# A two-layer transformer on one core: the second layer's q and k projected once, the rotary partner fetched by transfers

## The chip, the core and the metric

One core of a Trainium2 chip runs the whole program. The metric is the device time of one execution in microseconds; where several runs are compared, the median. Engines: PE (TensorE, matmuls and transposes), DVE (VectorE), ACT (ScalarE), POOL (GpSimd), SP (SyncE, which issues every DMA of this program). Each engine works through its own instructions strictly in order, and an instruction waits on semaphores that others raise.

## The reference

Two layers over x of 2 batches x 512 tokens x 256. Each layer is a layer norm, attention, a residual sum, a layer norm, a mixture of 16 experts and one shared expert, and a residual sum. Layer 0's attention has 16 heads of 128, layer 1's 16 heads of 16. What the change touches is the start of layer 1's attention:

```python
def rotate_half(x):
    half = x.shape[-1] // 2
    x1, x2 = (x[..., :half], x[..., half:])
    return jnp.concatenate([-x2, x1], axis=-1)

def apply_rope(x, base=BASE):
    ...
    return x * jnp.cos(emb) + rotate_half(x) * jnp.sin(emb)
```

q = x Wq + bq and k = x Wk + bk, both [2, 512, 256], both through apply_rope within each head of 16, then softmax(q k^T / 4) v and the output projection. Row i of a head and row i + 8 are each other's partners.

## The kernel before

All matmul inputs of the projections and experts are split into a high and a low part ("hi", "lo": ACT writes hi as a copy in the matmul's format, DVE or POOL writes the difference), and each product is three matmuls: hi by hi, lo by hi, hi by lo, over two chunks of 128 channels. So one projection of 128 output rows by 512 tokens is 6 matmuls of 128x128 weights by 512 columns.

The program is six stretches, one after the other: layer 0 attention, its 34 expert items ("rows", i = 0 to 33, `row_pe`, `row_act`, `row_dve`, `row_pool`: 17 experts for batch 0, then 17 for batch 1), layer 1 attention as 32 "steps" (`a1_pe`, `a1_act`, `a1_dve`, `a1_pool`, `a1_sp`), and its experts. The order on every engine is written out by hand; tables say at which row or step a side job stands.

A row i on PE is gate(i) and up(i) (6 matmuls of 512 columns each, L955 and L964) and down(i-2) (12 matmuls of 256 columns, L978). On ACT it is hid_high(i-1) (L1054), silu(i) (L1035), ew_high(i+2) (L1068), then side jobs. On DVE: hid_low(i-1), gated(i) (gu, L1153), side jobs. On POOL: weighted(i) (guw, L1118), ew_low(i+2) (L1102), side jobs. From row 20 on all rows use the same two PSUM banks for gate and up, so gate(i+1) waits until silu(i) has read its bank, and up(i+1) until gated(i) has.

Layer 1's q and k come in 8 groups g = (t, mt, h), with t = q or k, mt = a half of the 256 channels, h = the batch. Groups 0 to 3 (batch 0) are side jobs of rows 21 to 27, groups 4 to 7 (batch 1) of steps 4 to 11. The rotation is done by projecting twice: w1 holds q's weights, q's weights with each head's halves exchanged ("sw" = 1), the same for k, and v. For each group `group_pe` (L1517) runs 2 x 6 matmuls (L1527); `group_dve` (L1816) makes rc = (projection + bias) * cos and rs = (exchanged projection + bias) * sin out of PSUM; `rotated` on POOL (L1778) adds them to rr; `high` on ACT (L1688) and `low` (L1768; DVE for groups 0 to 3, POOL for 4 to 7) split rr; `stack` on SP (L1455) writes both to DRAM, from where `load` (L1459) brings pairs of heads back, stacked for the steps.

A step s of layer 1 attention: for each of 4 heads a slot j with one score matmul for the step (L1646, ks by qs, with 3 banks, so that matmul n waits for the exponential n - 2) and one maximum matmul for 7 steps later (L1550, read by DVE L1838); then 4 slots x 1 value matmul of the step before (L1616), which open the next step. ACT does the 4 exponentials (L1733) and then the step's side jobs. At s % 4 = 0 ACT also reads out the values, at s % 4 = 1 PE also turns maxima and values. Batch 1's layer norm is: `ln_stats(2, 1)` on DVE in step 0, rstd and xn on POOL (L265, L242), transposes by PE at the end of step STEP_T1 = 3, its groups from step 4.

Where the tables stand:

```python
ROW_GROUP = {21: ((0, 0), (0, 1)), 22: ((1, 0), (1, 1)), 23: ((2, 0), (2, 1)), 24: ((3, 0),), 25: ((3, 1),)}
ROW_V = {25: 0, 26: 1}
ROW_HIGH = {22: 0, 23: 1, 24: 2, 26: 3}
STEP_HIGH = {5: 4, 6: 5, 9: 6, 11: 7}
```

## Time and profile before

| | us |
|---|---|
| median of 3 runs | 871.23 |
| lowest and highest | 865.35, 877.39 |
| the profiled execution | 863.91 |
| its span, first to last instruction | 862.2 |
| PE busy in the span | 824.2 (96%) |
| DVE, ACT, POOL busy | 649.3, 525.4, 465.4 |

The span lies 1.7 us below the profiled execution's own time. A PE matmul's duration runs from its issue to its modelled end and overlaps the next one, so its price in a dense stretch is the distance between starts. "Idle before" in brackets is how long the engine stood before an instruction, and what released it.

### The profile page before, as it was taken

Reading aid. Unit: us, or ns where it says so; the run is one execution under the profiler, and the core shown is the slowest. Engines: PE = TensorE matmul, PEld = TensorE weight load, DVE = VectorE, ACT = ScalarE, POOL = GpSimd, SP = SyncE. Lnnn points to the kernel's source line nnn. Section 1 sums busy time; section 2 is a strip of 40 time slices with the busy share of each in tenths; the row PEclk is TensorE's granted clock in tenths of the full one; section 3 lists DMA queues with packets and bytes.
Section 4 is the critical chain, followed back from the end, with each engine's and each line's share of the span. In section 5 each row is a group of like instructions: output and inputs, shape, how many; then the busy total and the mean of one; then the engine's idle time right before and its main releaser. Section 6 shows DMA issues by size and latency. Waiting matters only on the chain.

```text
span 862.2 us, 14797 instructions
## 1 busy us (share of the span) xinstructions
PE 824.2 (96%) x4544; PEld 624.0 (72%) x4544; DVE 649.3 (75%) x1350; ACT 525.4 (61%) x1106; POOL 465.4 (54%) x399
## 2 busy tenths in 40 slices
PE   8899999999999999989998999999999889999997
PEld 6678788777878888866887888654444347888886
DVE  5898888899998888998386866868788544676553
ACT  4778788777878888773534442346566464454442
POOL 4555555665665556642666766533201326656774
PEclk9999999999999999999999999999999899999999
DMA  5232233332423223212764458312431132334441
GB/s 157 93 98 92 94 97 97 111 97 67 151 87 98 97 92 105 80 50 75 218 214 156 141 164 292 106 58 91 145 111 50 57 99 93 123 125 142 151 162 65
DMA packets 57442, 99.20 MB, mean 115 GB/s; under 512 B 8288, under 2 KB 19040, under 8 KB 57376
## 3 DMA queue, kind: packets, MB, share of 16 engines
q1 hardware_dynamic: 57376, 98.39, 35.6%
q8 instruction: 33, 0.54, 0.3%
q14 instruction: 33, 0.27, 0.1%
HBM read 71.88 MB, written 9.57 MB: 94 GB/s over the span
## 4 chain that ended last, share of the span: by engine, by line
PE 63%; issue 10%; POOL 10%; DVE 10%; ACT 4%; DMA 3%; SPq 1%; DVEq 0%; POOLq 0%; ACTq 0%
PE ps L978 10%; PE ps L964 10%; PE ps L955 9%; PE ps L321 6%; PE ps L386 5%; PE ps L332 4%; POOL q_sin L530 3%; PE ps L345 3%; PE ps L374 3%; PE ps L1646 3%; PE ps L1527 2%; PE ps L359 2%; POOL wqk_lo L517 2%; PE ps L1616 2%; DVE nm L1838 2%
## 5 line engine op out<-in xcount | busy, mean ns | idle before, releaser
L1102 POOL TENSOR_TENSOR ew_lo<-ew_raw,ew_hi 128x768 fp32r<-128x768 f32 x68 | 128.1, 1885 | 60.0 <-ACT ew_hi L1068 52.0
L1054 ACT ACTIVATE hid_hi<-guw 128x512 fp32r<-128x512 f32 x68 | 43.0, 632 | 156.1 <-POOL guw L1118 106.2
L1157 DVE TENSOR_TENSOR hid_lo<-guw,hid_hi 128x512 fp32r<-128x512 f32 x68 | 80.7, 1187 | 72.1 <-ACT hid_hi L1054 72.0
L1118 POOL TENSOR_TENSOR guw<-gu,cwb 128x512 f32<-128x512 f32 x61 | 80.4, 1319 | 91.1 <-issue 73.8
L530 POOL TENSOR_TENSOR q_sin<-q_sw,sin 128x512 f32<-128x512 f32 x64 | 83.4, 1311 | 52.5 <-DMA q_sw<-q_in 51.1
L1838 DVE TENSOR_REDUCE nm<-ps 128x1 f32<-128x512 f32 x128 | 81.3, 683 | 19.6 <-PE ps L1550 18.3
L1733 ACT ACTIVATE e<-ps 128x512 f32<-128x512 f32 x128 | 68.8, 601 | 35.4 <-PE ps L1646 35.2
L978 PE MATMUL ps<-ew_hi,hid_hi 128*128 128x256 f32 x272 | 78.3, 288 | 2.4 <-DVE hid_lo L1157 1.8
L509 DVE SCALAR_TENSOR_TENSOR w<-ex,rden,sgn 128x512 f32<-128x512 f32 (+3 forms) x128 | 78.0, 670 | 0.0
L437 ACT ACTIVATE ex<-sabs,nmax 128x512 f32<-128x512 f32 (+3 forms) x128 | 61.5, 551 | 27.1 <-DVE nmax L483 27.1
L978 PE MATMUL ps<-ew_lo,hid_hi 128*128 128x256 f32 x272 | 76.8, 282 | 0.0
L978 PE MATMUL ps<-ew_hi,hid_lo 128*128 128x256 f32 x272 | 76.8, 282 | 0.0
L332 PE MATMUL ps<-q_rot 128*128 128x512 f32 (+3 forms) x256 | 74.5, 433 | 1.1 <-DVE v L462 1.1
L386 PE MATMUL ps<-wT,v 128*128 128x512 f32 (+3 forms) x256 | 74.3, 433 | 1.0 <-ACT wT L422 1.0
L478 DVE TENSOR_TENSOR q_rot<-ps,q_sin 128x512 f32<-128x512 f32 x64 | 43.6, 688 | 39.5 <-POOL q_sin L530 24.6
L386 PEld LDWEIGHTS ps<-wT,v 128*128 128x128 f32 x256 | 46.3, 190 | 26.8 <-issue 16.6
L396 ACT ACTIVATE q_in<-ps,bqkv 128x512 f32<-128x512 f32 x64 | 43.8, 687 | 32.5 <-PE ps L321 32.4
L332 PEld LDWEIGHTS ps<-q_rot 128*128 128x128 f32 x256 | 43.4, 190 | 27.7 <-issue 16.6
L414 ACT ACTIVATE sgn<-ps 128x512 bf16<-128x512 f32 (+3 forms) x128 | 59.8, 468 | 0.0
L955 PE MATMUL ps<-xT_hi,ew_hi 128*128 128x512 f32 x136 | 55.7, 410 | 3.6 <-issue 3.6
L412 ACT ACTIVATE sabs<-ps 128x512 f32<-128x512 f32 (+3 forms) x128 | 58.7, 459 | 0.0
L1646 PE MATMUL ps<-qs,ks 50*128 50x512 f32 x128 | 51.5, 467 | 7.2 <-ACT e L1733 7.2
(189 smaller groups left out, 2397.3 us busy)
## 6 DMA issues: line engine op xcount, KB each, us to landing
ew_raw<-in_ew SPq DMA_DIRECT2D x68, 384.0 KB, 3.5
q_sw<-q_in SPq DMA_DIRECT2D x128, 128.0 KB, 2.0
cwb<-cw_dram SPq DMA_DIRECT2D x61, 256.0 KB, 3.7
wqk_raw<-in_wqk SPq DMA_DIRECT2D x32, 256.0 KB, 2.7
wv_raw<-in_wv SPq DMA_DIRECT2D x32, 128.0 KB, 2.6
wo_raw<-in_wo SPq DMA_DIRECT2D x32, 128.0 KB, 2.2
qs<-stk_q SPq DMA_DIRECT2D x16, 256.0 KB, 3.3
ks<-stk_k SPq DMA_DIRECT2D x16, 256.0 KB, 3.8
```

The lines of the kernel that those rows point to most:

```text
L332: pe.matmul(ps[:, bank, col:col + P * (qi + 1)], q_rot[:, par(1), 0, qi * P:(qi + 1) * P], q_rot[:, par(1), 1, 0:P * (qi + 1)], start=True ...
L386: last = pe.matmul(ps[:, 7, j * P:S], v0[:, slot_of(0), j, odd() * DH0:(odd() + 1) * DH0], wT[:, j, j * P:S], start=j == 0, stop=j == QT - ...
L509: dve.scalar_tensor_tensor(out=w[:, qi, ROW[qi]], in0=ex[:, qi, ROW[qi]], scalar=rden[:, qi:qi + 1], in1=sgn[:, par(1), qi, ROW[qi]], op0= ...
L530: pool.tensor_tensor(q_sin[:, t, :], q_sw[:, t, :], sin0[:, :], ALU.mult).then_inc(sem("q_sin"), 1)
L955: last = pe.matmul(ps[:, gu_pair(f, i)[0], :], ff[f].ew[pw][:, i % EW_SLOTS, c * P:(c + 1) * P], half_of((xT_hi, xT_lo)[px][:, c, :], h), ...
L964: last = pe.matmul(ps[:, gu_pair(f, i)[1], :], ff[f].ew[pw][:, i % EW_SLOTS, (DC + c) * P:(DC + c + 1) * P], half_of((xT_hi, xT_lo)[px][:, ...
L978: last = pe.matmul(ps[:, Y_BANK[f, h][t // 2], t % 2 * D:(t % 2 + 1) * D], ff[f].hid[px][:, i % 2, t * P:(t + 1) * P], ff[f].ew[pw][:, i % ...
L1102: pool.tensor_tensor(ff[f].ew[1][:, i % EW_SLOTS, :], ew_raw[:, i % RAW_SLOTS, :], fp(ff[f].ew[0][:, i % EW_SLOTS, :]), ALU.subtract).then ...
L1118: pool.tensor_tensor(ff[f].guw[:, i % 2, :], ff[f].gu[:, i % 2, :], ff[f].cwb[:, r % CWB_SLOTS, :], ALU.mult).then_inc(sem("guw"), 1)
L1157: dve.tensor_tensor(ff[f].hid[1][:, i % 2, :], ff[f].guw[:, i % 2, :], fp(ff[f].hid[0][:, i % 2, :]), ALU.subtract).then_inc(sem("hid_lo"), 1)
L1646: pe.matmul(ps[:, S_BANK[n % S_BANKS], :], ks[rows, slot_at, kt * P:(kt + 1) * P], qs[rows, slot_at, :], start=True, stop=True).then_inc(s ...
L1838: dve.tensor_reduce(nm1[:, quad % 2, col:col + 1], ps[:, BANK_OF["max", n], :], AX.X, ALU.max, negate=True).then_inc(sem("max"), 1)
```

## The change

- w1 holds 3 parts instead of 5 (q, k, v), loaded in 4 transfers instead of 6, split in rows 11, 13 and 15 instead of 11 to 19. `w1_parts` writes q's and k's columns interleaved (h i s), so that a row and its partner stand on neighbouring partitions; the tables cos, sin and b1 are loaded in that order, in 6 transfers instead of 3.
- Each group is projected once, by 6 matmuls. `evict` on ACT adds the bias and writes the group from PSUM to qe. `swap_halves` on SP copies qe to qw with even and odd partitions exchanged, in two transfers. `turned` on POOL makes rs = qw * sin. `group_dve` makes rc out of PSUM, and now waits for `evict`. `rotated` adds, on DVE in the rows and on POOL in the steps.
- Groups run in pairs: matmuls in rows 21 and 23 and in steps 3 and 6; `turned`, `rotated` and `high` of a pair one row later, in one row; in the steps `high` stands at the end of steps 5 and 8.
- v is projected in rows 22 and 24 instead of 25 and 26.
- `ln_stats(2, 1)` moves from step 0 to the end of the rows, STEP_T1 from 3 to 2.

```diff
-        ROW_GROUP = {21: ((0, 0), (0, 1)), 22: ((1, 0), (1, 1)), 23: ((2, 0), (2, 1)), 24: ((3, 0),), 25: ((3, 1),)}
-        ROW_V = {25: 0, 26: 1}
-        ROW_HIGH = {22: 0, 23: 1, 24: 2, 26: 3}
+        ROW_GROUP = {21: (0, 1), 23: (2, 3)}
+        ROW_TURN = {22: (0, 1), 24: (2, 3)}
+        ROW_V = {22: 0, 24: 1}
+        ROW_LOW = {23: (0, 1), 25: (2, 3)}
...
-        STEP_T1 = 3
+        STEP_T1 = 2
+        STEP_GROUP = {(3, 1): 4, (3, 3): 5, (6, 1): 6, (6, 3): 7}
+        STEP_HIGH = {5: (4, 5), 8: (6, 7)}
...
+        def swap_halves(sp, g):
+            sp.wait_ge(sem("qk1_ev"), g + 1)
+            wait(sp, "rs", g - 1)
+            for o in range(2):
+                sp.dma_start(qw[o:P:2, g % 2, :], qe[1 - o:P:2, g % 2, :]).then_inc(sem(f"qk1_sw{g % 2}"), 16)
...
             maxima(sp, 1)
             loads_after(sp, 0)
+            swap_halves(sp, 4)
+            swap_halves(sp, 5)
             maxima(sp, 2)
             stack(sp, 4)
             stack(sp, 5)
+            swap_halves(sp, 6)
+            swap_halves(sp, 7)
             sp.wait_ge(sem("stk_st"), 16 * 3 * 6)
             loads_after(sp, 1)
...
+        def evict(act, g):
+            t, mt, h = GROUPS1[g]
+            act.wait_ge(sem("qk1_ps"), g + 1)
...
+            act.activation(qe[:, g % 2, :], ps[:, BANK_OF["qk", g], :], ACT.Identity,
+                           bias=b1[:, 2 * t, mt:mt + 1]).then_inc(sem("qk1_ev"), 1)
...
-            if i in ROW_HIGH:
-                high(act, ROW_HIGH[i])
+            for g in ROW_TURN.get(i, ()):
+                high(act, g)
+            for g in ROW_GROUP.get(i, ()):
+                evict(act, g)
...
-        def rotated(pool, g):
-            pool.wait_ge(sem("rs"), 2 * (g + 1))
-            wait(pool, "qk1_hi", g - 1)
+        def turned(pool, g):
+            pool.wait_ge(sem(f"qk1_sw{g % 2}"), 32 * (g // 2 + 1))
+            wait(pool, "rr", g - 1)
+            pool.tensor_tensor(rs[:, g % 2, :], qw[:, g % 2, :], sin1[:, :], ALU.mult).then_inc(sem("rs"), 1)
+
+        def rotated(eng, g):
+            eng.wait_ge(sem("rs"), g + 1)
+            eng.wait_ge(sem("qk1_cos"), g + 1)
+            wait(eng, "qk1_hi", g - 1)
...
-            for g in range(4, 8):
-                rotated(pool, g)
-                low(pool, g)
-                if g == 5:
+            for g in range(4, 8, 2):
+                for step in (turned, rotated, low):
+                    step(pool, g)
+                    step(pool, g + 1)
+                if g == 4:
                     x_bias(pool, 1)
...
+                for g in ROW_LOW.get(i, ()):
+                    low(dve, g)
+                for g in ROW_GROUP.get(i, ()):
+                    group_dve(dve, g)
                 if i in ROW_V:
                     v_dve(dve, ROW_V[i])
-                if i in ROW_HIGH:
-                    low(dve, ROW_HIGH[i])
+                for g in ROW_TURN.get(i, ()):
+                    rotated(dve, g)
```

ACT in the rows, before, from row 22's hid_hi on (hid_hi, gu and ew_hi are one row's three jobs, qk_hi<-rr is `high`):

```order
L1054 ACTIVATE hid_hi<-guw_124 128x512 [waits y,guw]
L1035 ACTIVATE gu_123<-ps 128x512 [waits guw,gate]
L1068 ACTIVATE ew_hi<-ew_raw 128x768 [waits y,ew_ld0]
L1688 ACTIVATE qk_hi<-rr 128x512 [waits rr]
L1054 ACTIVATE hid_hi<-guw_124 128x512 [waits y,guw]
L1035 ACTIVATE gu_123<-ps 128x512 [waits guw,gate]
L1068 ACTIVATE ew_hi<-ew_raw 128x768 [waits y,ew_ld1]
L1688 ACTIVATE qk_hi<-rr 128x512 [waits rr]
```

and of the changed kernel, from row 22's hid_hi on (qe is what `evict` writes):

```order
L1054 ACTIVATE hid_hi<-guw_126 128x512 [waits y,guw]
L1035 ACTIVATE gu_125<-ps 128x512 [waits guw,gate]
L1068 ACTIVATE ew_hi<-ew_raw 128x768 [waits y,ew_ld0]
L1713 ACTIVATE qk_hi<-rr 128x512 [waits rr] x2
L1054 ACTIVATE hid_hi<-guw_126 128x512 [waits y,guw]
L1035 ACTIVATE gu_125<-ps 128x512 [waits guw,gate]
L1068 ACTIVATE ew_hi<-ew_raw 128x768 [waits y,ew_ld1]
L1705 ACTIVATE qe<-ps,b_99 128x512 [waits qk1_sw0,qk1_ps]
L1705 ACTIVATE qe<-ps,b_99 128x512 [waits qk1_sw1,qk1_ps]
```

Before, one `high` closed each of rows 22 and 23. Now row 22 closes with two and row 23 with two `evict`s; row 24 closes with the other two `high`s, row 25 with nothing.

POOL in the rows, before, rows 21 and 22 (guw is `weighted`, ew_lo is `ew_low`, rr is `rotated`):

```order
L1118 TENSOR_TENSOR guw_124<-gu_123,cwb_122 128x512 [waits hid_lo,gu,cwb_ld1]
L1102 TENSOR_TENSOR ew_lo<-ew_raw,ew_hi 128x768 [waits ew_hi_act]
L1778 TENSOR_TENSOR rr<-rc,rs 128x512 [waits rs]
L1118 TENSOR_TENSOR guw_124<-gu_123,cwb_122 128x512 [waits hid_lo,gu,cwb_ld2]
L1102 TENSOR_TENSOR ew_lo<-ew_raw,ew_hi 128x768 [waits ew_hi_act]
L1778 TENSOR_TENSOR rr<-rc,rs 128x512 [waits rs]
```

and of the changed kernel, rows 21 to 23 (rs is `turned`):

```order
L1118 TENSOR_TENSOR guw_126<-gu_125,cwb_124 128x512 [waits hid_lo,gu,cwb_ld1]
L1102 TENSOR_TENSOR ew_lo<-ew_raw,ew_hi 128x768 [waits ew_hi_act]
L1118 TENSOR_TENSOR guw_126<-gu_125,cwb_124 128x512 [waits hid_lo,gu,cwb_ld2]
L1102 TENSOR_TENSOR ew_lo<-ew_raw,ew_hi 128x768 [waits ew_hi_act]
L1814 TENSOR_TENSOR rs<-qw,sin_98 128x512 [waits qk1_sw0]
L1814 TENSOR_TENSOR rs<-qw,sin_98 128x512 [waits qk1_sw1]
L1118 TENSOR_TENSOR guw_126<-gu_125,cwb_124 128x512 [waits hid_lo,gu,cwb_ld0]
```

One operation in each of rows 21 to 23 and 25 has become two in row 22 and two in row 24, and the sum is DVE's.

ACT in the steps, before, from the second half of step 4 to the first half of step 8 (e is an exponential, zst the read-out, nmT the turned maxima):

```order
L1733 ACTIVATE e_157<-ps 128x512 [waits pv1,st_ps] x6
L1693 ACTIVATE nmT<-ps 32x128 [waits nm_st0,nmT_ps]
L1688 ACTIVATE qk_hi<-rr 128x512 [waits stk_st,rr]
L1733 ACTIVATE e_157<-ps 128x512 [waits pv1,st_ps] x4
L1688 ACTIVATE qk_hi<-rr 128x512 [waits rr]
L1733 ACTIVATE e_157<-ps 128x512 [waits pv1,st_ps] x6
```

and of the changed kernel, steps 3 to 7:

```order
L1770 ACTIVATE e_159<-ps 128x512 [waits pv1,st_ps] x4
L1705 ACTIVATE qe<-ps,b_99 128x512 [waits qk1_sw0,qk1_ps]
L1705 ACTIVATE qe<-ps,b_99 128x512 [waits qk1_sw1,qk1_ps]
L1770 ACTIVATE e_159<-ps 128x512 [waits pv1,st_ps] x2
L1727 ACTIVATE zst<-ps 128x512 [waits pv1]
L1770 ACTIVATE e_159<-ps 128x512 [waits pv1,st_ps] x6
L1718 ACTIVATE nmT<-ps 32x128 [waits nm_st0,nmT_ps]
L1713 ACTIVATE qk_hi<-rr 128x512 [waits stk_st,rr]
L1713 ACTIVATE qk_hi<-rr 128x512 [waits rr]
L1770 ACTIVATE e_159<-ps 128x512 [waits pv1,st_ps] x4
L1705 ACTIVATE qe<-ps,b_99 128x512 [waits qk1_sw0,qk1_ps]
L1705 ACTIVATE qe<-ps,b_99 128x512 [waits qk1_sw1,qk1_ps]
```

Two `evict`s now stand between the exponentials of steps 3 and 4 and of steps 6 and 7, and two `high`s behind those of step 5 (and of step 8), where single `high`s stood behind steps 5, 6, 9 and 11.

## Rows read from the trace of the kernel before

**Rows 1.** The page: busy time of each engine, its share of the span, instructions.

```profile
PE 824.2 (96%) x4544; PEld 624.0 (72%) x4544; DVE 649.3 (75%) x1350; ACT 525.4 (61%) x1106; POOL 465.4 (54%) x399
```

**Rows 2.** Windows: expert rows 21 to 26, attention steps 1 to 11.

```profile
core 0: us, PE busy (x) PEld busy (x) DVE busy (x) ACT busy (x) POOL busy (x), PEclk, DMA share, GB/s
...
487.44:526.95 39.51, 39.51 (x219) 34.15 (x218) 24.25 (x29) 14.69 (x24) 26.77 (x18) 1.00 0.62 198
...
576.75:623.25 46.50, 43.72 (x248) 20.35 (x247) 37.03 (x64) 26.75 (x53) 18.09 (x14) 1.00 0.33 106
```

**Rows 3.** Timeline of PE, row 22 (start, duration, engine, line).

```profile
494.56 0.39 PE L955 MATMUL ps<-xT_hi,ew_hi 128*128 128x512 f32 x1
...
497.35 0.39 PE L1527 MATMUL ps<-xT_hi,w_hi 128*128 128x512 f32 x1
...
500.13 0.28 PE L978 MATMUL ps<-ew_hi,hid_hi 128*128 128x256 f32 x1
...
501.57 0.39 PE L955 MATMUL ps<-xT_hi,ew_hi 128*128 128x512 f32 x1
```

**Rows 4.** Timeline of ACT and POOL, rows 22 and 23.

```profile
496.15 0.60 ACT L1035 ACTIVATE gu<-ps 128x512 f32<-128x512 f32 x1 [0.70 <-PE ps L955]
...
498.44 1.29 POOL L1118 TENSOR_TENSOR guw<-gu,cwb 128x512 f32<-128x512 f32 x1 [1.82 <-issue]
...
499.69 1.86 POOL L1102 TENSOR_TENSOR ew_lo<-ew_raw,ew_hi 128x768 fp32r<-128x768 f32 x1
```

**Rows 5.** Timeline of POOL and DVE, row 21: two operations that meet.

```profile
489.12 1.86 POOL L1102 TENSOR_TENSOR ew_lo<-ew_raw,ew_hi 128x768 fp32r<-128x768 f32 x1
...
489.87 1.66 DVE L1157 TENSOR_TENSOR hid_lo<-guw,hid_hi 128x512 fp32r<-128x512 f32 x1 [0.66 <-ACT hid_hi L1054]
```

**Rows 6.** Layer 0's exchange; DMA issues (KB each, us to landing).

```profile
224.51 0.69 ACT L396 ACTIVATE q_in<-ps,bqkv 128x512 f32<-128x512 f32 x1 [0.70 <-PE ps L321]
...
227.60 2.55 POOL L530 TENSOR_TENSOR q_sin<-q_sw,sin 128x512 f32<-128x512 f32 x2 [0.49 <-DMA q_sw<-q_in]
...
q_sw<-q_in SPq DMA_DIRECT2D x128, 128.0 KB, 2.0
...
w_raw<-in_w SPq DMA_DIRECT2D x6, 256.0 KB, 5.9
```

**Rows 7.** Timeline of PE, attention steps (L1616 opens each step).

```profile
584.76 1.09 PE L277 MATMUL ps<-ident,xn 128*128 128x128 f32 x8
...
588.01 0.50 PE L1527 MATMUL ps<-xT_hi,w_hi 128*128 128x512 f32 x1
...
589.61 0.50 PE L1646 MATMUL ps<-qs,ks 50*128 50x512 f32 x1
...
598.04 1.07 PE L1616 MATMUL ps<-e,vx 128*32 128x512 f32 x8
...
600.65 1.07 PE L1616 MATMUL ps<-e,vx 128*32 128x512 f32 x8
...
638.26 1.06 PE L1616 MATMUL ps<-e,vx 128*32 128x512 f32 x8
...
641.53 1.06 PE L1616 MATMUL ps<-e,vx 128*32 128x512 f32 x8
...
644.86 1.07 PE L1616 MATMUL ps<-e,vx 128*32 128x512 f32 x8
```

**Rows 8.** Timeline of DVE and POOL, step 0: norm of batch 1.

```profile
574.81 1.39 DVE L231 BATCH_NORM_STATS2 stats<-x 128x6 f32<-128x256 f32 x4
...
576.76 1.02 POOL L265 TENSOR_TENSOR rstd<-vareps,minus_half 128x4 f32<-128x4 f32 x1 [11.35 <-DVE vareps L236]
```

**Rows 9.** Timeline of DVE in step 24, and two windows there.

```profile
671.44 4.26 DVE L1843 TENSOR_TENSOR nm_s<-nm 128x16 fp32r<-128x16 f32 x1
...
671.00:675.00 4.00, 2.37 (x14) 0.67 (x12) 3.90 (x2) 3.03 (x6) 4.00 (x3) 0.99 0.00 0
...
675.00:681.80 6.80, 5.66 (x17) 2.34 (x21) 2.76 (x6) 1.19 (x3) 0.67 (x1) 0.50 0.28 84
```

124 lines of the change are left out of this document (67 added, 57 removed).

## The prediction

> **What bounds the kernel now.** I read the page's busy line first, then the windows of the two stretches that the change touches, then PE's timeline in them, then the engines behind PE. PE is busy for 96% of the span [rows 1]. In rows 21 to 26 it has no idle time at all: 39.51 us busy of 39.51 [rows 2]. So there a matmul removed is time won, as long as nothing else becomes late. In the attention steps 1 to 11 PE is busy for 43.72 of 46.50 us, with DVE at 37.03 and ACT at 26.75 [rows 2]: PE still leads, with less room. A row of two projections lasts 501.57 - 494.56 = 7.01 us, of which gate and up take 2.79, the twelve projection matmuls 2.78 and the downs 1.44 [rows 3]. One 512-column matmul is thus worth 2.78 / 12 = 0.232 us.
>
> **What is removed.** 8 groups x 6 matmuls = 48, worth 11.1 us at 0.232. They fall in two halves. In the rows, 24 x 0.232 = 5.6 us. The two v jobs (12 matmuls of 256 columns, as the downs, 1.44) only change places. In the steps a group of six takes 589.61 - 588.01 = 1.60 us [rows 7], so four are worth 6.4.
>
> **Rows 21 to 26: what is late next.** Before, one `high` closed a row on ACT and found its input ready. Now a pair goes through weighted, ew_low, `turned` twice (POOL), `rotated` twice (DVE) and `high` twice (ACT) within one row, and ACT cannot take up the next row's silu before it. For row 22: POOL ends weighted and ew_low at 499.69 + 1.86 = 501.55 [rows 4]. Two `turned` at layer 0's rate for the same operation (2.55 for two, [rows 6]) end at 504.1. `rotated` meets a lock: hid_lo, a subtraction of two SBUF operands on DVE, met a POOL operation that ended at 490.98 and itself ended at 491.53, 0.55 later, after 1.66 us [rows 5]. So the first `rotated` ends at 504.65, 0.55 behind the second `turned`, and the second at 505.2. Two `high`s and hid_high (0.6 each) end at 506.3 with some overlap, silu (0.60, [rows 4]) at 506.85, 12.3 us after the row's start. Gate of row 24 needs that silu. Rows 22 and 23 on PE last 7.01 - 2.78 + 1.44 = 5.67 and 7.01, so row 24 starts at 507.2: covered, by 0.4 us. The same chain starts again in row 24, where 5.67 and an empty row of 4.23 lie in front of row 26's gate: 9.9 us against 12.3, a stall of 2.4. It grows because DVE reaches row 24 late: in row 23 it makes two `low`s, each held by a POOL operation in the same way [rows 5], and two rc's behind `evict`, which moves gated(24) some 2 us. I take 4.5 us (ends: 2.4 without that lag, 5 with a slower exchange), and 0.6 more for ew_low(27), which waits for row 25's weighted. Rows: 5.6 - 4.5 - 0.6 = 0.5 us saved instead of 5.6. The exchange itself is hidden there: `evict` of group 1 ends at about 494.0, in layer 0 the data was there 227.60 - 225.20 = 2.4 us after the eviction [rows 6], and POOL asks at 501.5. At 5.9, the slowest kind of transfer in the list [rows 6], it is hidden too.
>
> The lock between DVE and POOL is also what the Trainium skill describes (SBUF — State Buffer, section "SBUF: two separate sides"): a DVE operation with two SBUF inputs and a reading POOL operation exclude each other for a whole instruction. By it `rotated` on DVE beside `turned` on POOL is not parallel work; rows 5 agree with their 1.66 us. Without the lock the chain would be 0.5 us shorter and DVE not late in row 24: a stall of 1.9 us instead of 4.5, and 863.7 instead of the sum below.
>
> **Steps 1 to 11.** Without stalls I add the new steps up from rows 7: six plain ones at 600.65 - 598.04 = 2.61 (15.7), two with a read-out at 641.53 - 638.26 = 3.27 (6.5), two with turned maxima at 644.86 - 641.53 = 3.33 (6.7), one with four more transposes, estimated at 2.9, the layer norm's transposes 1.1, four groups 6.4. Sum 39.3 against 46.50 [rows 2], 7.2 saved; the removed groups are 6.4 of it, the rest is a wait for a load that the earlier stacking should end.
>
> Against that stand the new waits on ACT. (a) `evict` of groups 5 and 7 (0.69 us, the shape of layer 0's q_in, [rows 6]) stands ahead of the next step's first exponential, which PE's score matmul needs: 0.35 us each, 0.7. (b) `high` of groups 4 and 5 at the end of step 5. Counted from the start of step 4: `evict` done at 0.8, exchange landed at 3.8 (2.4 in rows 6, plus the queue on SP), second `turned` 5.1, two `rotated` 7.6, second `high` 8.2, first exponential of step 6 at 8.8. PE wants it at 8.0: 0.8 us. (c) `high` of groups 6 and 7 at the end of step 8, two steps after the pair's, which are only 2.6 + 0.35 + 3.3 = 6.2 us long: by the same count the exponential comes at 8.7, and PE wants it at 7.2: 1.5 us. DVE waits for `evict` too, with maxima behind it, but four PSUM banks lie between. Steps: 7.2 - 0.7 - 0.8 - 1.5 = 4.2 us saved.
>
> **Small things.** ln_stats(2, 1) leaves step 0, where it kept POOL waiting 11.35 us [rows 8]. Its 2 us (1.39 for the sums, [rows 8], and the small operations) go to the end of the rows, ahead of two maxima that PE does not need for four slots: nothing there, about 0.2 won at the maxima of step 0. Two splits of w1 leave ACT and DVE in rows 17 and 19, where PE hardly waits: 0 to 0.3. The interleaved split of q and k has no row; it lies under experts with the same element count: 0, at most 1 us if strides slow it. Three more issues on SP in row 14 stand ahead of an expert's load that is used three rows later: 0.
>
> **Sum.** 0.5 + 4.2 + 0.2 = 4.9 us. The profiled execution took 863.91, so 859.0 in its terms. It lies 7.3 below the median of the three runs, 871.23; in their terms 866.3.
>
> **Rivals.**
> 1. The stalls are not there: ACT's queue has slack that I miss. Then rows and steps give 5.6 + 7.2 less a little, 12: 859.3. For it: PE without idle time in rows 21 to 26 [rows 2] with ACT at 14.69 of 39.51. Against: ACT's slack is no help to what stands behind a wait in its own queue.
> 2. PE's clock falls in row 26. In step 24 a DVE operation was held 4.26 us; PE was busy 2.37 of 4.00 us there, and in the next 6.80 us the granted clock was 0.50, the lower level of 1.2 GHz [rows 9]. A stall of 4.5 us in row 26 has the same form. Some 4.4 of such 6.8 us would fall on matmuls at half speed and cost 2.2, of which 0.6 hides the wait for ew_low(27): 1.6 less saved, and with a second such gap in step 9 3.3: 869.6 at the far end. The Trainium skill has the same rule (TensorE: Matmul & The Clock Gate, section "Why this matters for your kernels"): idle gaps between bursts return the array to the lower clock. Rows 9 agree, with 0.50.
> 3. The exchange is slow in the steps, and the kernel becomes slower. If it lands 7 us after `evict` (5.9 from issue, as w_raw's loads, [rows 6], plus issue) and not 3, ACT's `high` behind steps 5 and 8 holds all exponentials 4 us longer, twice: 8 us, and two idle gaps of 5 us bring the clock down, 3 us more: 11 - 4.9 = 6.1 slower, 877.3. It turns the sign when landing takes more than about 5.4 us. Against it: q_sw lands in 2.0 [rows 6], and the steps have less DMA work (share 0.33) than the rows (0.62) [rows 2].
>
> **Chances.** The forecast (saved 2.5 to 7 us) 0.5, rival 1 0.2, rival 2 0.15, rival 3 0.12, anything else 0.03. The range, from rival 1 with its interval to rival 3 with most of its, and the scatter of runs, 857.5 to 877. About 2% can be told from no change for this kernel. 2% is 17.4 us: more than all matmuls removed and every wait won (about 13), so faster by over 2% gets only the runs' scatter, 0.03; slower by over 2% needs rival 3 with more than twice its price, 0.04; within 2% 0.93.
>
> **What would show it.** In the new profile: ACT idle in front of `high` in rows 22 and 24, about 7 us each time, released by DVE's rr; PE idle before row 26's gate for 2 to 5 us; idle in front of the score matmuls of steps 6 and 9; 48 projection matmuls of q and k instead of 96; half clock near row 26 or not. PE dense through row 26 with row 27's gate 5.6 us earlier would refute my main step; exchanges landing over 5 us would point to rival 3.

## The result, and the profile after

The changed kernel takes 878.64 us (median of 10 runs, 868.51 to 882.45) against 870.41 (10 runs, 864.55 to 877.39): ratio 1.0107, 95% interval 1.0063 to 1.0151. It is slower by about 1%, 8.2 us by the medians. The ratio is taken from the fast executions; three of the changed kernel's ten were slow ones, over 1.5% above its fastest, and without them its median is 876.35. The profiled execution took 876.35 us with a span of 874.2, against 863.91 and 862.2. These two lie 12.4 us apart, 4 more than the medians, since the profiled execution of the kernel before was quicker than any of the ten.

The page's busy line (compare [rows 1]) shows the 48 matmuls gone from PE (4496 for 4544) and its share two points lower:

```profile
PE 824.9 (94%) x4496; PEld 622.6 (71%) x4496; DVE 647.7 (74%) x1344; ACT 529.6 (61%) x1112; POOL 470.3 (54%) x403
```

PE is busy as long as before with fewer matmuls. Windows of the changed kernel tell why: first the two that answer to [rows 2] (rows 21 to 26, steps 1 to 11, from the same instructions), then three stretches at half clock.

```profile
core 0: us, PE busy (x) PEld busy (x) DVE busy (x) ACT busy (x) POOL busy (x), PEclk, DMA share, GB/s
488.64:531.51 42.87, 36.06 (x195) 31.15 (x194) 25.46 (x29) 16.94 (x28) 25.38 (x17) 0.92 0.63 202
581.24:635.50 54.26, 45.75 (x225) 18.88 (x224) 37.61 (x60) 29.94 (x59) 19.14 (x15) 0.78 0.35 117
...
522.70:529.50 6.80, 4.21 (x10) 3.37 (x11) 5.45 (x7) 4.71 (x8) 3.38 (x2) 0.50 0.98 358
597.80:604.60 6.80, 6.08 (x29) 2.05 (x21) 6.24 (x10) 4.03 (x9) 5.42 (x5) 0.50 0.01 2
618.30:635.30 17.00, 12.55 (x49) 5.33 (x49) 7.75 (x13) 8.82 (x18) 5.71 (x5) 0.50 0.33 105
```

The 12.0 us between the spans lie so: 1.2 before row 21 (1.5 up to row 0, in code that the change leaves alone and where the clock fell twice for 3.4 us, then 0.3 won), 42.87 - 39.51 = 3.4 in rows 21 to 26, nothing from row 27 to step 1, 54.26 - 46.50 = 7.8 in steps 1 to 11, nothing behind them.

**The rows.** Timeline of the changed kernel in rows 23 to 26:

```profile
511.48 1.41 SPq L1457 DMA_DIRECT2D stk_k<-qk_lo  x1
513.00 5.10 SPq L1463 DMA_DIRECT2D qw<-qe  x4
...
519.85 2.48 POOL L1814 TENSOR_TENSOR rs<-qw,sin 128x512 f32<-128x512 f32 x2 [2.56 <-DMA qw<-qe]
521.14 2.34 DVE L1824 TENSOR_TENSOR rr<-rc,rs 128x512 f32<-128x512 f32 x2 [6.49 <-POOL rs L1814]
522.91 1.23 ACT L1713 ACTIVATE qk_hi<-rr 128x512 fp32r<-128x512 f32 x2 [10.37 <-DVE rr L1824]
524.57 0.58 ACT L1035 ACTIVATE gu<-ps 128x512 f32<-128x512 f32 x1
525.29 0.76 PE L955 MATMUL ps<-xT_hi,ew_hi 128*128 128x512 f32 x1 [6.80 <-ACT gu L1035]
```

Read it upwards: the gate of row 26 (L955) waits 6.80 us for silu, silu stands behind `high` (L1713), which waits 10.37 us for `rotated`, that for `turned`, and that for the exchange, which SP issues behind the stacks of groups 0 and 1 and which has landed by 519.85. Row 26 then runs at half clock and takes 6.22 us instead of 4.23. So: -5.6 for the matmuls, +6.8 for the stall, +2.0 for the clock; that is 3.2 of the 3.4.

**The steps.** Timeline of the changed kernel in steps 8 and 9:

```profile
608.82 1.80 SPq L1457 DMA_DIRECT2D stk_k<-qk_lo  x1
609.59 0.69 ACT L1705 ACTIVATE qe<-ps,b 128x512 f32<-128x512 f32 x1 [1.56 <-PE ps L1543]
610.72 4.37 SPq L1463 DMA_DIRECT2D qw<-qe  x4
616.63 2.49 POOL L1814 TENSOR_TENSOR rs<-qw,sin 128x512 f32<-128x512 f32 x2 [9.40 <-DMA qw<-qe]
620.36 0.63 ACT L1713 ACTIVATE qk_hi<-rr 128x512 fp32r<-128x512 f32 x1 [4.87 <-POOL rr L1824]
622.12 1.07 ACT L1770 ACTIVATE e<-ps 128x512 f32<-128x512 f32 x2
622.75 0.79 PE L1662 MATMUL ps<-qs,ks 50*128 50x512 f32 x1 [5.71 <-ACT e L1770]
```

SP issues both exchanges from 610.72 on, behind the stacks. Group 6's lands at 616.6, 8.5 us behind its `evict`; `evict` of group 7 ends at 610.28 and its exchange lands at 617.4, 7.1 us later. ACT holds step 9's exponentials behind `high` of 6 and 7; PE waits 5.71 us. Step 9 takes 10.32 us (3.33 for a step of its kind), and 10 and 11, at half clock, 5.20 and 4.00 instead of 2.9 and 2.6. Step 5 shows another wait, on DVE:

```profile
597.25 1.28 POOL L1814 TENSOR_TENSOR rs<-qw,sin 128x512 f32<-128x512 f32 x1 [0.37 <-DMA qw<-qe]
598.48 2.50 POOL L1824 TENSOR_TENSOR rr<-rc,rs 128x512 f32<-128x512 f32 x2
598.55 1.24 DVE L1887 TENSOR_TENSOR nm_s<-nm 128x16 fp32r<-128x16 f32 x1
599.82 1.19 DVE L1889 TENSOR_TENSOR nm_s<-nm,nm_s 128x16 fp32r<-128x16 f32 x1
601.07 0.40 PE L1572 MATMUL ps<-ident,nm_s 128*32 128x128 f32 x1 [0.71 <-DVE nm_s L1889]
```

Two products of 16 columns, 0.17 us each where POOL is idle, take 1.24 and 1.19 beside POOL's operations, and PE's next instruction needs them. Step 5 takes 5.90 instead of 3.33. PE stands 0.71 us of that; the rest is at half clock, which began at 597.8, ahead of both products. Where step 5 ran at full clock with the same order (rows_high_late, high67_at_10_loads, loads_first, warm_26), PE stood 1.8 us there and the step took 5.17 to 5.20.

### The profile page after: what moved, and what is told of

The parts are those of the page before. It is cut to its first block and busy times, and to the rows that moved or that the text cites. A ratio compares the mean times of both kernels' runs of the same rounds, so it can differ in the third digit from the quotient of the medians.

```text
span 874.2 us, 14742 instructions
## 1 busy us (share of the span) xinstructions
PE 824.9 (94%) x4496; PEld 622.6 (71%) x4496; DVE 647.7 (74%) x1344; ACT 529.6 (61%) x1112; POOL 470.3 (54%) x403
## 5 line engine op out<-in xcount | busy, mean ns | idle before, releaser
L1157 DVE TENSOR_TENSOR hid_lo<-guw,hid_hi 128x512 fp32r<-128x512 f32 x68 | 78.6, 1156 | 71.8 <-ACT hid_hi L1054 71.6
L1662 PE MATMUL ps<-qs,ks 50*128 50x512 f32 x128 | 55.3, 497 | 13.4 <-ACT e L1770 13.3
L955 PE MATMUL ps<-xT_hi,ew_hi 128*128 128x512 f32 x136 | 56.3, 414 | 10.5 <-ACT gu L1035 6.8
L1662 PEld LDWEIGHTS ps<-qs,ks 50*128 50x128 f32 x128 | 22.7, 200 | 59.9 <-ACT e L1770 47.8
```

Source lines behind the costliest of these rows:

```text
L955: last = pe.matmul(ps[:, gu_pair(f, i)[0], :], ff[f].ew[pw][:, i % EW_SLOTS, c * P:(c + 1) * P], half_of((xT_hi, xT_lo)[px][:, c, :], h), ...
L1157: dve.tensor_tensor(ff[f].hid[1][:, i % 2, :], ff[f].guw[:, i % 2, :], fp(ff[f].hid[0][:, i % 2, :]), ALU.subtract).then_inc(sem("hid_lo"), 1)
L1662: pe.matmul(ps[:, S_BANK[n % S_BANKS], :], ks[rows, slot_at, kt * P:(kt + 1) * P], qs[rows, slot_at, :], start=True, stop=True).then_inc(s ...
```

## The experiments

Each is compared with the kernel before, run on the same chip; the changed kernel's ratio is 1.0107. The changed kernel itself was run in one set only, in which the kernel before had a median of 870.41, against 865.05 to 866.60 in the sets below; of the kernels made from it, all_three, all_four and all_five alone have intervals that lie wholly under its own. Since the clock also falls in places that no edit touches (last section), two stretches of each trace stand beside the ratio: row 21's gate to row 33's, and the start of step 2 to that of step 14.

| kernel | ratio (95%) | rows 21-33 | steps 2-14 |
|---|---|---|---|
| before | 1 | 72.80 | 53.49 |
| changed | 1.0107 (1.0063-1.0151) | 76.12 | 61.30 |
| rows_high_late | 1.0140 (1.0082-1.0198) | 73.44 | 62.71 |
| steps_high_late | 1.0292 (1.0241-1.0343) | 76.28 | 72.73 |
| both_high_late | 1.0245 (1.0184-1.0307) | 73.67 | 72.49 |
| no_exchange | 1.0046 (1.0003-1.0089) | 73.15 | 56.05 |
| rows_turn_25 | 1.0061 (1.0027-1.0095) | 73.47 | 61.71 |
| high67_at_10 | 1.0126 (1.0044-1.0207) | 76.02 | 61.52 |
| high67_at_10_loads | 1.0033 (0.9991-1.0074) | 76.13 | 58.01 |
| swap_pool_queue | 1.0099 (1.0058-1.0140) | 76.07 | 60.90 |
| rows_sum_25 | 1.0068 (1.0032-1.0104) | 71.61 | 59.82 |
| loads_first | 1.0060 (1.0027-1.0092) | 76.54 | 53.61 |
| sum_after_nm | 1.0165 (1.0117-1.0214) | 76.55 | 61.94 |
| all_three | 1.0008 (0.9975-1.0041) | 71.59 | 54.45 |
| before_less | 0.9950 (0.9922-0.9979) | 68.12 | 53.88 |
| warm_26 | 1.0159 (1.0097-1.0220) | 74.95 | 65.86 |
| all_four | 0.9989 (0.9959-1.0020) | 71.24 | 57.24 |
| all_five | 0.9995 (0.9961-1.0030) | 71.04 | 53.73 |
| before_less_early | 0.9917 (0.9883-0.9951) | 68.12 | 48.85 |
| before_early | 0.9967 (0.9936-0.9998) | 72.81 | 52.18 |

How far one trace's stretch can be trusted is seen where an edit leaves its code alone. Rows 21 to 33 took 76.02 to 76.55 us in the six kernels whose edit lies in the steps only. Steps 2 to 14 took 59.82 to 62.71 in three whose edit lies in the rows only (warm_26, with its clock down in steps 0 to 2, 65.86): in kernels made from the changed one, a difference under 3 us there says little.

**First: are the highs only too early?** rows_high_late:

```diff
-            for g in ROW_TURN.get(i, ()):
+            for g in ROW_TURN.get(i - 1, ()):
                 high(act, g)
```

> ScalarE makes the two high parts of groups 0, 1 in row 23 and of groups 2, 3 in row 25, a row later than in the changed kernel; nothing else moves. Theory A (the highs stand too early on ScalarE): in the changed kernel's trace the gate matmul of row 27 stands 4.6 us later than before the change and that of row 25 0.1 us earlier, so 4.7 us are lost to the wait for row 24's highs, half of it stall (TensorE idle 6.80 us in front of row 26's gate), half of it clock at 0.5 for 6.8 us. Then this kernel is 4 to 5 us faster than the changed one, TensorE has no wait over 1 us in front of row 26's gate and the granted clock stays at full speed there. Theory B (fewer matmuls keep TensorE thin, so the clock falls with or without a stall): the clock falls near row 26 all the same and the gain is 2 to 3 us. Theory C (the highs only wait in another row): the stall of 4 to 7 us stands before row 25's or 27's gate, gain under 1 us.

Measured: row 24's gate to row 28's 25.88 us (28.55 in the changed kernel), so 2.7 won, and half clock from 520.5 all the same. The wait had gone to the next engine, as its timeline shows:

```profile
516.93 2.51 POOL L1814 TENSOR_TENSOR rs<-qw,sin 128x512 f32<-128x512 f32 x2 [2.57 <-DMA qw<-qe]
518.25 2.34 DVE L1824 TENSOR_TENSOR rr<-rc,rs 128x512 f32<-128x512 f32 x2 [6.33 <-POOL rs L1814]
521.11 0.68 DVE L1153 TENSOR_TENSOR gu<-gu,ps 128x512 f32<-128x512 f32 x1
521.84 0.80 PE L964 MATMUL ps<-xT_hi,ew_hi 128*128 128x512 f32 x1 [3.60 <-DVE gu L1153]
```

DVE's product of gate and up stands behind `rotated`. A is half right, C names the rest. The ratio does not show the 2.7; the two intervals leave room for it.

This run's steps are those of the changed kernel, and they show a wait that the changed kernel's own trace hides:

```profile
636.10 0.51 PE L1566 MATMUL ps<-ks,qs 48*128 48x512 f32 x2 [1.96 <-DMA ks<-stk_k]
```

The loads behind the stacks of groups 6 and 7 are late for step 13, which takes 9.73 us instead of 4.96. In the changed kernel PE comes later to it, since steps 10 and 11 ran at half clock (5.20 and 4.00 us, here 3.51 and 2.73). The three other kernels with unedited steps show 8.10, 6.19 and 10.34. So 4.96 is no measure for the experiments below, and part of the half clock behind step 9 covers this wait.

steps_high_late has this edit, and both_high_late has it beside that of rows_high_late:

```diff
-        STEP_HIGH = {5: (4, 5), 8: (6, 7)}
+        STEP_HIGH = {6: (4, 5), 10: (6, 7)}
```

> ScalarE makes the highs of groups 4, 5 behind the exponentials of step 6 (5 in the changed kernel) and those of groups 6, 7 behind step 10's (8). Theory A: from step 9's value matmuls to step 12's the changed kernel takes 19.5 us and the kernel before 13.6; the 5.9 us are the 5.71 us that TensorE waits for step 9's exponentials behind the highs of groups 6, 7 and the half clock after it, less the two projections gone there. Then this kernel is 5 to 7 us faster than the changed one and steps 9 to 12 run at full clock. Theory B (thin TensorE): half clock of 15 us or more stays between steps 5 and 12, gain 2 to 3 us, the stall's share alone. Theory C (the wait moves to a later step): TensorE waits 3 us or more for exponentials in step 11, gain under 2 us.

> The two edits together. Theory A: the two gains add, 9 to 12 us under the changed kernel, which is 1 to 3 us under the kernel before. Theory B: 4 to 6 us under the changed kernel, still 2 to 4 us above the kernel before. Theory C: under 3 us.

All three theories fall: steps 2 to 14 took 11.4 us longer than in the changed kernel. `high` of groups 4 and 5 came at 608.5, so their stacks were issued until 615.8, the exchange of groups 6 and 7 from 615.9, the loads at 620.6, and step 9's maxima waited 4.8 us for these loads. What stands on SP is one chain: stacks of one pair, exchange of the next, loads. A `high` that is late for ACT's good is late for all of it.

**Second: the exchange itself.** no_exchange leaves the exchange out:

```diff
-            pool.wait_ge(sem(f"qk1_sw{g % 2}"), 32 * (g // 2 + 1))
+            pool.wait_ge(sem("qk1_ev"), g + 1)
...
-            pool.tensor_tensor(rs[:, g % 2, :], qw[:, g % 2, :], sin1[:, :], ALU.mult).then_inc(sem("rs"), 1)
+            pool.tensor_tensor(rs[:, g % 2, :], qe[:, g % 2, :], sin1[:, :], ALU.mult).then_inc(sem("rs"), 1)
...
-                swap_halves(sp, g)
```

> Leaves out the exchange of partner rows: the sine product reads the evicted rows themselves, and the 32 transfers and their waits are gone; all else as in the changed kernel. Theory D (the exchange is what is late): in row 24 GpSimd's sine product then starts 2.6 us earlier, so the stall before row 26's gate falls from 6.8 to about 4.3 us; in step 8 it starts 5.7 us earlier (at about 611 instead of 616.6), so the highs are ready when ScalarE comes to them and step 9's stall of 5.7 us and its half clock are gone: 7 to 9 us faster in all. Theory A' (the engines' chain of sine product, sum and high is too long by itself): both stalls stay over 3 us, gain 2 to 4 us. Theory B: gain 2 us or less, half clock remains.

The row 26 stall is 4.2 us (forecast of D 4.3; my prediction, with the exchange hidden, 4.5), and step 9 takes 4.33 us instead of 10.32. The exchange is worth 3.0 us in the rows and 5.3 in the steps, 8.2 together, where theory D expected 7 to 9; the ratios give 5.3 us, with overlapping intervals. So it is the traces that show D. Step 5's two products took 0.18 and 0.17 us here. Step 13 took 9.71 us, as long as it can take with unedited steps.

swap_pool_queue issues the exchanges of groups 4 to 7 from POOL:

```diff
-            swap_halves(sp, 4)
-            swap_halves(sp, 5)
-            swap_halves(sp, 6)
-            swap_halves(sp, 7)
...
-                for step in (turned, rotated, low):
+                for step in (swap_halves, turned, rotated, low):
```

> The exchanges of groups 4 to 7 are issued by GpSimd, which waits for them anyway, instead of SyncE, where those of groups 6, 7 stand behind the stacks of groups 4, 5; the rest is the changed kernel. Theory S: the exchange of group 6 starts at its eviction (608.0 on the changed kernel's scale instead of 610.7) and that of group 7 at 610.3, so the sums are ready 2 to 4 us earlier and step 9's stall of 5.7 us falls to 2 to 4: 2 to 5 us faster than the changed kernel. Rival Q (the time is in the transfer itself and in GpSimd's issue, not in the queue it stands in): stall over 5 us, within 1.5 us of the changed kernel or slower.

Timeline of POOL in it:

```profile
606.56 1.12 POOL L1463 DMA_DIRECT2D qw<-qe  x2
608.72 1.09 POOL L1463 DMA_DIRECT2D qw<-qe  x2 [1.04 <-ACT qe L1701]
613.42 1.27 POOL L1810 TENSOR_TENSOR rs<-qw,sin 128x512 f32<-128x512 f32 x1 [3.61 <-DMA qw<-qe]
617.16 1.26 POOL L1810 TENSOR_TENSOR rs<-qw,sin 128x512 f32<-128x512 f32 x1 [2.46 <-DMA qw<-qe]
```

Issued 4 us earlier (these steps run 1.3 us ahead of the changed kernel's), the two exchanges land at 613.3 and 617.1, where the changed kernel has 616.6 and 617.4: group 6's gains, group 7's does not, and PE's stall in step 9 is 6.88 us, over the 5 of rival Q. The DMA issues of POOL (KB each, us to landing) in two windows, 592 to 598 with no stack on its way, and 606 to 618 beside the stacks of groups 4 and 5:

```profile
qw<-qe POOLq DMA_DIRECT2D x4, 128.0 KB, 2.3
```

```profile
qw<-qe POOLq DMA_DIRECT2D x4, 128.0 KB, 5.5
```

The same transfer from the same queue takes 3.2 us longer beside the stacks (six transfers of 256 KB for a pair). So most of its lateness comes with the stacks, and leaving SP's queue does not cure it. What in the stacks slows it is not told apart: the DMA engines' busy share was 0.63 in the changed kernel at that time, not 1.

**Third: loads behind stacks.** high67_at_10 has the first hunk, high67_at_10_loads both:

```diff
-        STEP_HIGH = {5: (4, 5), 8: (6, 7)}
+        STEP_HIGH = {5: (4, 5), 10: (6, 7)}
...
             stack(sp, 6)
-            stack(sp, 7)
             loads_after(sp, 2)
+            stack(sp, 7)
```

> Only the highs of groups 6, 7 move, from behind step 8's exponentials to behind step 10's. Theory S (one queue carries exchange, stacks and loads in one order): step 9's 5.7 us wait for exponentials goes, but the loads issued at step 12 follow the six transfers of 256 KB of groups 6, 7 directly and land late, as in the runs where step 13 took 9.7 us instead of 5.0; so 1 to 4 us faster than the changed kernel, with step 13 at 9 to 12 us. Rival R (only the order on ScalarE matters): step 13 stays at 5 us and the gain is 6 to 9 us.

> The run before with one more edit: the transfers to DRAM of group 7 are issued behind the loads of step 12, as in the kernel before. Theory S: step 13 takes 5 us again and the whole is 6 to 9 us faster than the changed kernel, that is 0 to 2 us slower or faster than the kernel before. Rival R: no difference to the run before it.

Step 9 fell to 5.43 us, step 12 rose to 7.13 and step 13 to 10.29, and nothing was won: R falls. For S step 13 says less than it seems, since with no edit in the steps it also took up to 10.34. With group 7's stacks behind the loads step 13 is 8.28. Still too long: the loads went at 630.9, behind group 6's stacks. loads_first puts both behind (highs of 6, 7 behind step 10 again):

```diff
+            loads_after(sp, 2)
             stack(sp, 6)
             stack(sp, 7)
-            loads_after(sp, 2)
```

> Highs of groups 6, 7 behind step 10 and SyncE issues the loads of step 12 ahead of the stacks of both groups 6 and 7 (with only group 7's behind them step 13 took 8.3 us: the loads were issued at 630.9, behind group 6's stacks). Theory S: the loads are issued 2 us earlier with no stack's bytes in front, step 13 takes 5 to 6 us, and from step 3's value matmuls to step 14's it takes 50 to 51.5 us (changed kernel 57.7, with group 7 alone behind the loads 53.2, kernel before 50.9): 7 to 9 us faster than the changed kernel. Rival (another wait stands there, or step 17 waits for groups 6, 7's stacks instead): over 53 us, or a step of 5 us or more among steps 16 to 19 that took 3.3 before.

Steps 3 to 14 took 49.97 us and step 13 4.96, at full clock and with no wait for loads: S is shown for this stretch. The ratio gives 4 us, not 7 to 9; the profile has 43 us of half clock, 3.4 of them in steps 3 to 14.

**Fourth: the small products.** sum_after_nm:

```diff
                 for step in (turned, rotated, low):
+                    if step is rotated:
+                        pool.wait_ge(sem("nm_lo"), 1 + g // 2)
                     step(pool, g)
```

> The changed kernel with one wait more: GpSimd starts the sums of groups 4, 5 (6, 7) only after VectorE's two small products of the negated maxima of step 4 (8) are done. In the changed kernel these took 1.24 and 1.19 us in step 5 beside GpSimd's sums, against 0.17 each where GpSimd was idle. Theory L (a GpSimd operation on two SBUF tensors holds VectorE's): the second of the two takes 0.2 to 0.4 us again, the first at most what is left of the sine product before it; TensorE's maxima transpose comes 1 us or more earlier in step 5, which takes 4.5 to 5 us instead of 5.9; 1 to 3 us faster than the changed kernel. Rival N (the small products are late for another reason): both stay near 1.2 us, no gain; or the later sums push the highs out and it is slower.

Step 5's products took 0.18 and 0.17 us and step 5 3.33 instead of 5.90: L, with 1.9 us for the wait (5.2 at full clock) and 0.7 for the clock. Then step 6 waits for the first time, 0.81 us for its exponentials behind the highs, and takes 6.66 instead of 6.08:

```profile
603.55 0.49 PE L1662 MATMUL ps<-qs,ks 50*128 50x512 f32 x1 [0.81 <-ACT e L1770]
```

In step 9 POOL's wait stood too late (products 1.10 and 1.19, beside `turned`). The kernel was not faster; its step 13 took 10.22 us, as in others whose step 13 was not touched.

**Fifth: the rows' order.** rows_turn_25 (highs a row late too, stacks of groups 2, 3 in row 27) and rows_sum_25:

```diff
-        ROW_TURN = {22: (0, 1), 24: (2, 3)}
-        ROW_LOW = {23: (0, 1), 25: (2, 3)}
+        ROW_TURN = {22: (0, 1), 25: (2, 3)}
+        ROW_LOW = {23: (0, 1), 26: (2, 3)}
```

> Row 24's sine products and sums of groups 2, 3 move to row 25, their highs to row 26 ahead of that row's evictions (groups 0, 1: row 23), their lows to row 26 and their transfers to DRAM to row 27. In the run that moved the highs alone a row down, the wait moved from ScalarE to VectorE: VectorE held row 25's product of gate and up 3.6 us behind a sum that waited 6.3 us for GpSimd's sine products and these 2.6 us for the exchange. Theory V (the exchange's landing and the sine products reach into row 25's work, so whichever engine holds the next step stalls): with another row between, no engine waits over 1.5 us in front of the gates of rows 25 to 27, the clock stays at full speed, and from row 24's gate to row 27's it takes 18.4 to 19 us as before the change (23.1 in the changed kernel, 20.3 with the highs alone moved): 4 to 5 us faster than the changed kernel. Rival W (the sums on VectorE and sine products on GpSimd hold each other wherever they stand): a wait of 2 to 4 us and a half clock in row 25 or 26, gain 1 to 3 us.

```diff
         ROW_TURN = {22: (0, 1), 24: (2, 3)}
+        ROW_SUM = {22: (0, 1), 25: (2, 3)}
-        ROW_LOW = {23: (0, 1), 25: (2, 3)}
+        ROW_LOW = {23: (0, 1), 26: (2, 3)}
...
+            for g in ROW_GROUP.get(i, ()):
+                swap_halves(sp, g)
             for g in ROW_STACK.get(i, ()):
                 stack(sp, g)
-            for g in ROW_GROUP.get(i, ()):
-                swap_halves(sp, g)
```

> In row 23 the exchange of groups 2, 3 is issued ahead of the stacks of groups 0, 1; the sums of groups 2, 3 on VectorE move from row 24 to row 25 (their sine products stay with GpSimd in row 24), highs and lows to row 26, stacks to row 27; groups 0, 1 have their highs in row 23. Theory X (within one row the chain product of gate and up, weighting, expert lows, two sine products, two sums is about 8 us by VectorE's and GpSimd's order, longer than a row of 5.5, and the sums stand at its end in VectorE's order; with the sums a row later VectorE comes to them when the sine products are done): row 24's gate to row 28's takes 24 to 25 us (before the change 23.8, changed kernel 28.6, sine products moved to row 25 25.9), no wait over 1.5 us of TensorE there and no half clock: 3.5 to 5 us faster than the changed kernel. Rival Y (the row pays wherever the two engines' five operations stand): 26 us or more, half clock again.

Both free the gates: PE waits at most 0.32 us before those of rows 25 to 27, so neither W nor Y holds, which saw VectorE and GpSimd in each other's way wherever they stand. What is left stands in row 27, before its maxima; first rows_turn_25, then rows_sum_25:

```profile
528.94 0.80 PE L1566 MATMUL ps<-ks,qs 48*128 48x512 f32 x2 [3.74 <-DMA ks<-stk_k]
```

```profile
524.49 0.50 PE L1567 MATMUL ps<-ks,qs 48*128 48x512 f32 x2 [2.38 <-DMA ks<-stk_k]
```

These are row 25's loads, which PE now reaches before they land; in the changed kernel the stall of row 26 hid them. V and X were right about the engines and had no term for this wait and the half clock near it (6.8 and 3.4 us). From row 24's gate to row 28's it is 25.91 and 24.06 us, the second in X's range. For the gates it matters that a wait does not stand in the row in which its input is made.

**Sixth: together.** all_three joins rows_sum_25, loads_first and sum_after_nm.

> The three edits together: sums of groups 2, 3 in row 25 with the exchange ahead of the stacks, loads ahead of the stacks of groups 6, 7 and their highs behind step 10, and GpSimd's wait ahead of the sums. If the gains add (4, 8 and 1 to 2 us), 11 to 14 us under the changed kernel, 2 to 5 us under the kernel before (ratio to it 0.994 to 0.998). If the clock falls all the same (half clock of 20 us or more in rows and steps), 5 to 8 us under the changed kernel and no faster than before.

all_four issues row 25's loads in row 24 and puts POOL's wait for groups 6, 7 ahead of `turned`; all_five moves group 7's projection from (6, 3) to (8, 2).

```diff
-        ROW_LOADS = {25: (0, 4), 28: (4, SLOTS)}
+        ROW_LOADS = {24: (0, 4), 28: (4, SLOTS)}
...
-                    if step is rotated:
+                    if (step, g) in ((rotated, 4), (turned, 6)):
```

> The run of the three edits together with two changes: the first loads of tiles (row 25's) are issued in row 24, since TensorE waited 2.4 us for them in row 27 with half clock behind it; and GpSimd's wait for VectorE's small products stands ahead of the sine products of groups 6, 7 instead of their sums (for groups 4, 5 ahead of the sums as there), since in step 9 the small products took 0.83 and 1.19 us beside the sine products. Expected: row 24's gate to row 28's 21 to 22.5 us (24.0), step 9 5.0 to 5.5 us (6.7) and no half clock in either place: 3 to 5 us under that run, ratio to the kernel before 0.995 to 0.998. If the waits there are only handed on (to the loads of step 9, to the highs), the ratio is 0.999 to 1.003.

> The run of the four edits with group 7's projection in step 8, slot 2, where the kernel before had one, instead of step 6, slot 3; its exchange behind the loads of step 8, its high behind step 11. In the kernel before, step 8's projection (1.7 us) stood on TensorE between the score that frees the tiles' slots and step 9's maxima, which wait for the loads' 3.2 us; cutting most of it (40 matmuls left out) made step 8 1.2 us shorter and step 9 2.3 us longer. Theory M (a removed or moved matmul in front of a landing is worth nothing, and the landing is the bound): steps 6 to 10 together take 1.2 to 2.5 us less than in the run of the four edits (24.2 us from step 6's value matmuls to step 11's), the wait for the loads in step 9 under 0.8 us and no half clock there; ratio to the kernel before 0.995 to 0.998. Rival Z (the wait there has another cause): the step with the projection grows by 1.6 us and nothing shrinks beyond the 1.6 us that leave step 6; ratio 0.998 to 1.002.

About 1% is taken back: all_three's interval lies wholly under the changed kernel's, 8.6 us by the ratios, not the 11 to 14 of the added gains. But none beats the kernel before. all_four won 2.7 us up to row 28 (PE waited 1.1 us for row 27's loads instead of 2.4) and gave 2.4 back by row 33; its step 9, expected at 5.0 to 5.5 us, took 7.00, with 2.0 us of wait for loads. all_five's step 9 still waited 2.0 us for its loads: Z.

**Seventh: was the removed work worth its price?** before_less is the kernel before:

```diff
-            for j in range(3 * DC):
+            for j in range(1 if sw else 3 * DC):
...
-                                 half_of((xT_hi, xT_lo)[px][:, ch, :], h), start=j == 0, stop=j == 3 * DC - 1)
+                                 half_of((xT_hi, xT_lo)[px][:, ch, :], h), start=j == 0, stop=sw == 1 or j == 3 * DC - 1)
```

> The kernel before, with the second projection of each group (the partner's) cut from 6 matmuls to its first: 40 of TensorE's matmuls are left out, evictions, products, sums, highs, stacks and their places stay. It prices the removed work alone. Theory P (the prediction's price, 0.232 us of path for each): 40 x 0.232 = 9.3 us faster than the kernel before. Rival K (other engines and the loads set the pace of part of these rows and steps, and a thinner TensorE loses clock): 3 to 6 us faster, with the steps that had two projections shorter by less than 1.3 us for each projection cut, or half clock where the kernel before has none.

40 matmuls gave 0.50% (0.21 to 0.78), 4.3 us: K. In rows 21 to 33 20 of them gave 4.68 us, the full 0.232 each. In steps 3 to 14 the other 20 gave 50.88 - 50.10 = 0.8: step 9 grew from 6.44 to 8.75, with 1.94 us of wait for loads instead of 1.06 and 3.4 us of half clock behind it. SP's waits tell what it stood on; first the kernel before, then before_less, steps 6 to 10:

```profile
SPq L1459 <- DMA stk_k<-qk_lo: 5.8, 1, 5.8
```

```profile
SPq L1459 <- DMA stk_k<-qk_lo: 5.7, 1, 5.7
```

and PE's side, timeline of before_less:

```profile
603.16 0.57 SPq L1455 DMA_DIRECT2D stk_k<-qk_lo  x1
609.47 0.33 SPq L1459 DMA_DIRECT2D qs<-stk_q  x1
612.82 0.50 PE L1550 MATMUL ps<-ks,qs 48*128 48x512 f32 x2 [1.94 <-DMA ks<-stk_k]
```

Group 5's last stack is issued at 603.2 and lands at 609.5; the loads, which wait for it, land at 612.8. Two legs of one way through DRAM, 9.7 us: PE can only come sooner and wait longer.

before_less_early and before_early start that way a step sooner:

```diff
-        STEP_T1 = 3
-        STEP_GROUP = {(4, 1): (4, 0), (4, 3): (4, 1), (5, 1): (5, 0), (5, 3): (5, 1), (7, 2): (6, 0), (8, 2): (6, 1),
-        STEP_HIGH = {5: 4, 6: 5, 9: 6, 11: 7}
+        STEP_T1 = 2
+        STEP_GROUP = {(3, 1): (4, 0), (3, 3): (4, 1), (4, 1): (5, 0), (4, 3): (5, 1), (7, 2): (6, 0), (8, 2): (6, 1),
+        STEP_HIGH = {4: 4, 5: 5, 9: 6, 11: 7}
...
-            maxima(sp, 2)
             stack(sp, 4)
+            maxima(sp, 2)
             stack(sp, 5)
```

> The kernel before with 40 of the partner projections' matmuls left out, as before_less, and with groups 4, 5 a step earlier (their four projections in steps 3 and 4 instead of 4 and 5, their highs behind steps 4 and 5, batch 1's norm a step earlier as in the change, group 4's stacks issued ahead of step 5's maxima). Theory T (the bound of steps 3 to 9 is group 5's way through DRAM: in the kernel before its projection ends at 598.0, its last low is issued at 602.3 and lands at 608.8, where SyncE, which waited 5.8 us for that landing, issues the loads that step 9's maxima wait for until 612.25; whatever TensorE saves ahead of that it waits off there): with the way 3.4 us earlier, step 9 takes 5.0 to 5.6 us (8.75 with the matmuls cut alone, 6.44 before), and from step 3's value matmuls to step 14's it takes 46 to 47.5 us (50.1 cut alone, 50.9 before): 2.5 to 4 us faster than before_less, ratio to the kernel before 0.989 to 0.993. Rival U (TensorE waits there for slots or the clock, not for that landing): step 9 stays over 7 us, 49 us or more, ratio 0.994 to 0.997.

> The same a step earlier with all matmuls in place: the output is the reference's. Theory T: step 9's wait of 1.06 us for loads goes and step 9 takes 5.0 to 5.4 us, from step 3 to step 14 49.2 to 50 us (50.9): 1 to 1.7 us faster than the kernel before, ratio 0.997 to 0.999. Rival U: no difference or slower, ratio 0.999 to 1.003.

T. Steps 2 to 14 took 48.85 us with the matmuls cut (53.88 without the shift, 1.2 of it clock in step 2) and 52.18 with all of them (53.49). Timeline of before_early:

```profile
604.17 0.72 SPq L1456 DMA_DIRECT2D stk_k<-qk_lo  x1
609.84 0.33 SPq L1460 DMA_DIRECT2D qs<-stk_q  x1
...
613.99 0.73 PE L1551 MATMUL ps<-ks,qs 48*128 48x512 f32 x2
```

No wait stands at step 9's maxima. before_early leaves nothing out and comes out ahead of both kernels: 0.9967 (0.9936 to 0.9998), some 3 us, of which the steps' stretch shows 1.3. The interval only just stays under 1, and those of before_less and before_less_early overlap; what shows T is step 9 (5.30 and 5.59 us) and the stretch. And the matmuls of the steps are worth more only now: 52.18 - 48.85 = 3.3 us for 20.

**Eighth: wait or clock?** warm_26 is the changed kernel with work in the stall:

```diff
+            if (f, i) == (0, 26):
+                bank_wait(pe, "max", 0)
+                warm(pe, 24, BANK_OF["max", 0], xT_hi[:, 0, :])
```

> The changed kernel with 24 matmuls of 128x512 more, whose results nobody reads, ahead of the waits of row 26's gate on TensorE: 24 x 0.232 = 5.6 us of work inside the stall of 6.8 us. It tells the stall's wait from its clock. Theory G (the clock falls because TensorE is idle): no half clock between 520 and 530, and from row 25's gate to row 28's it takes 20.5 to 21.8 us (changed kernel 22.9): 1.1 to 2.4 us less. Rival H (the clock falls for what came before the stall): half clock of 3.4 to 6.8 us there as before and 22.5 to 24 us. The whole within 3 us of the changed kernel either way.

```profile
517.04 5.62 PE L666 MATMUL ps<-xT_hi 128*128 128x512 f32 x24
524.19 0.48 PE L958 MATMUL ps<-xT_hi,ew_hi 128*128 128x512 f32 x1 [1.53 <-ACT gu L1038]
```

No half clock there, and row 25's gate to row 28's 21.72 us instead of 22.88: G. So the clock fell for the stall and cost 1.2 to 2.0 us beside its 6.8. The whole was not faster: in its profile the clock fell at 576.2 for 17 us, and step 13 took 10.34.

## Why the prediction was wrong

I said 866.3 us, 4.9 saved; it is 8.2 lost by the medians, and 878.64 lies above my range of 857.5 to 877.

- **The price of the removed matmuls.** In the rows 0.232 us each holds (4.68 us for 20, before_less). In the steps "7.2 saved" fails. I had seen the wait for a load before and called it something "that the earlier stacking should end". It was the bound: the way of group 5 through DRAM. In the changed kernel its projection ends 6.2 us behind the start of step 3 instead of 15.9, but exchange, `high` in pairs and six stacks in a row end it later: the last stack is issued 21.2 us behind the start of step 3 (608.82 - 587.61), before 20.2, and the loads at 28.3 instead of 26.7.
- **"The exchange itself is hidden there".** For groups 0 and 1 it was. For groups 2 and 3 I took the same without looking at row 23's SP, where the stacks of the first pair stand ahead: it had landed by 519.85, 9.9 us behind `evict`. Without the exchange the stall is 4.2, near my 4.5; with it 6.8. The mechanism of row 26 (ACT's `high` ahead of silu, 5.67 and an empty row against the chain) was right, down to row 22, which waited 7.14 us on ACT and did not stall.
- **Step (c), 1.5 us in step 9**, took an exchange landed 3 us behind `evict`. For group 7 it was 7.1, because the pair before was being stacked, and PE waited 5.71 us. That is rival 3: price 6.1 us slower for landings of 7 us, measured 8.2. I gave it 0.12 and argued against it with the mean DMA share of the steps, 0.33. While the pair was exchanged it was nearly twice that, as a window of the changed kernel shows:

```profile
610.70:616.60 5.90, 5.17 (x32) 1.83 (x32) 5.11 (x9) 4.08 (x9) 0.00 (x0) 1.00 0.63 225
```

  The price had one term of mine (the hold, twice) where there was one hold, one lock and more clock, so that its 6.1 comes near the measured 8.2 is in part luck.
- **Step (b), 0.8 us in step 6**, did not show: step 6 took 6.08 us against 5.8, no PE instruction waited there, and its first 1.2 us were at half clock. The wait in step 5, which I did not have, had covered it. Without that wait it is there, 0.81 us (sum_after_nm).
- **The lock.** I priced it for the rows and not for nm_s in step 5, though [rows 9] show the same operation held 4.26 us in step 24. Cost 1.9 us in step 5 at full clock, 2.6 with the half clock of the changed kernel (sum_after_nm), and 0.6 of it comes back in step 6.
- **The clock (rival 2)** came as described in row 26 (2.0 us, forecast 2.2) and behind step 9, where the half clock lasted 17 us, not 6.8. There it also covers step 13's wait for loads, a third bound that my sum had nowhere.
- **Small things**: 0 from row 27 to step 1, where I had 0.2.

Rows: 0.5 saved forecast, 3.4 lost. Steps: 4.2 saved forecast, 7.8 lost. Of these 15.9 us 8.2 go with the exchange and what follows on it (no_exchange), the lock of step 5 among them, since its products are quick there too. The other 7.7 (clock, pairs of highs, late loads) are not told apart. That the three repaired orders together only reach the kernel before is the last point: 11.1 us of matmuls were never all to be had.

## What to carry to other kernels

Before pricing a removed matmul by its duration, look for the transfer that the next wait of that stage ends on, and follow it back: if the chain to it does not start earlier, the saving is waited off. Here a transfer landed late when other transfers were issued ahead of it, on its own queue or on another (2.3 us alone, 5.5 beside the stacks), so take a landing from a moment with the same traffic and not from a mean. And a step that waits belongs, in every engine's order, behind work that is due first.

## What the runs showed of the hardware

The granted clock also fell where no edit had touched anything: in 7 of the 20 profiles it went to 0.50 for 6.8 to 17 us beginning between 570 and 581, in row 33 or steps 0 to 2, in the others not, with nearly the same instructions there. Windows of before_less:

```profile
560.00:570.10 10.10, 9.26 (x54) 6.37 (x52) 5.64 (x9) 4.23 (x7) 1.29 (x1) 1.00 0.08 7
...
570.10:583.80 13.70, 13.70 (x44) 4.67 (x42) 7.54 (x21) 4.65 (x10) 6.75 (x6) 0.50 0.25 86
```

PE was busy for 92% of the 10 us ahead of it. Such a fall costs 3 to 6 us (steps 1 and 2 of all_four took 4.50 and 5.97 us instead of 2.74 and 3.62). Executions of one kernel differ in the same way: in the 13 of the kernel before that stand beside no_exchange, the mean granted clock goes from 1.000 at 860.36 us to 0.980 at 876.56. That would explain why single edits worth 2 to 3 us in a stretch did not show in ratios. What decides it stays open.

One issue on SP takes 0.43 us for a load, 0.5 to 0.6 for a half of the exchange and 0.6 for a stack when nothing is on its way. Behind stacks a half of the exchange took up to 2.05 us (groups 2 and 3), a stack up to 1.80 and a load 0.85 (634.19): a full queue takes the engine's time too.
